# Cross-attention: the copy of the attended values out of PSUM moves from behind the fourth exponential of a step to behind the first exponential of the next

## The chip, the cores and the metric

The kernel runs on one core of one Trainium2 chip. The metric is the device time in microseconds (us); lower is better. The engines are called as in the profile: PE is TensorE, with PEld for its weight loads; ACT is ScalarE, DVE is VectorE, POOL is GpSimd, and SP is SyncE, which here only issues DMAs.

## The reference, cut to what matters

A decoder layer over 32 blocks of 128 positions and 512 features, in three parts: self-attention, cross-attention, feed-forward. The change touches the second alone:

```
qh = q.reshape(B, 8, 16, 512); kh = k.reshape(...); vh = v.reshape(...)
qk = einsum('bhdq,bhdl->bhql', qh, kh) * 0.25
ret = einsum('bhql,bhdl->bhdq', softmax(qk), vh)
x = layernorm(x + gamma * ret)
```

So each block has 8 heads of 512 queries, 512 keys and depth 16. The kernel never divides by the softmax's sum at this place. It computes exp(score - maximum), multiplies that by the values with a row of ones beside them, and the row of ones gives the sum.

## The kernel before

`self_attention`, `cross_attention` and `feed_forward` are three program blocks, one after the other: the second begins when all engines have left the first. In `cross_attention` every engine runs its own list of instructions, in order, and semaphores tie the lists together. [...]

A block of the batch is called t (0 to 31). It is worked off in 8 steps n = 0 to 7 (`STEPS`), four heads in steps 0 to 3 (group g = 0) and four in steps 4 to 7 (g = 1); within a group each step takes a quarter of the keys. `pairs` unrolls t = 0, 1 and t = 30, 31, and runs t = 2 to 29 in a hardware loop of 14 turns with two blocks in each, in which the values that waits compare with are computed from a register.

In step n the engines do this:

- PE (`step`, L1020 to L1036), in this order: a pair of score tiles k = 4n and 4n+1 into the PSUM buffers `e_ps` (two matmuls of L1017); the raw scores for the maximum of block t+1 (L981, two matmuls into `m_ps`); the third score tile; two more matmuls of L981; the fourth score tile; then `products(n - 1)` (L1002, eight records), which multiplies the exponentials of the step before by the values and adds into the one PSUM buffer `av_ps`. There are three buffers `e_ps` for four tiles a step (`bank_of`), so the pair of step n+1 waits until the third exponential of step n is done, and the fourth tile of step n waits until the first exponential of step n is done.
- ACT (`step`, L894 to L910): four exponentials of 128x512 (L901), from `e_ps` to `prob` in SBUF.
- DVE: two maxima (L926) over `m_ps`; at n = 5 also the reciprocals of the block before (L932, L936).

Steps 0 and 4 end with more. Behind `products`, PE transposes the maxima of one group into `m_ps` (L988); ACT copies them out (`evict_max`, L892); PE's next matmul of L981 waits for that copy, and so do POOL's splits (L852, L855) and the DMAs (L862) that bring the maxima to the stack `xs` for scores four steps later. ACT then copies the attended values of the group that has just been finished from `av_ps` to `heads` (`copy_heads`, L886). SP stores `heads` and later loads the sums for the reciprocals.

One wait counts above all:

```
if lc == 0 and not (first and g == 0):
    pe.wait_ge(heads_done, 2 * b + g)
```

`products` for the first quarter of a group overwrites `av_ps` and so waits for `copy_heads` of the group before. It stands at the end of PE's step 1 and of step 5. What `copy_heads` itself waits for is the `products` call at the end of PE's step 0 or 4, the last one of that group, and the store of the same `heads` buffer one block earlier.

Of the kernel before, what the change touches and what calls it, by code (L numbers as in the profile page):

```python
# [633 lines left out]
def cross_attention(nc, NB, t_in, scratch, ffn_stage, ffn_abs):  # L634
# [13 lines left out]
    def bank_of(k):  # L648
        return k % 3

    with ExitStack() as ctx:
# [62 lines left out]
        def pairs(eng, pair):  # L714

            pair(0, True, False)
            if NB > 4:
                with eng.Fori(1, NB // 2 - 1) as s:
                    pair(s, False, False)
            pair(NB // 2 - 1, False, True)  # L720
# [159 lines left out]
        @block.scalar  # L880
        def _(act):
            def copy_heads(b, g, first=False):
                act.wait_ge(av_done, STEPS * b + KC * (g + 1))
                if not first:
                    act.wait_ge(heads_st[g], 16 * b)
                act.activation(heads[g][:, :], av_ps[:, :], ACT.Copy).then_inc(heads_done, 1)  # L886

            def evict_max(b, g, first=False):
                act.wait_ge(mt_done, 2 * b + g + 1)
                if not first:  # L890
                    act.wait_ge(part_done, 4 * b + 2 * g - 2)
                act.activation(neg_max[g][:, :], m_ps[0][0:XG * KC, 0, 0:P], ACT.Copy).then_inc(neg_done, 1)  # L892

            def step(t, first, second=False, last=False):  # L894
                for n in range(STEPS):
                    for j in range(XG):
                        k = XG * n + j
                        act.wait_ge(score_done[k % 2], PAIRS * t + k // 2 + 1)
                        if j == 0 and not (first and n < 2):
                            act.wait_ge(av_done, STEPS * t + n - 1)  # L900
                        act.activation(prob[k % 8][:, :], e_ps[bank_of(k)][:, :], ACT.Exp, scale=0.25).then_inc(  # L901
                            exp_done, 1)
                    if n == 0:
                        evict_max(t, 1, first=first)
                    if n == 4 and not last:
                        evict_max(t + 1, 0)
                    if n == 0 and not first:
                        copy_heads(t - 1, 1, first=second)
                    if n == 4:
                        copy_heads(t, 0, first=first)  # L910

            def pair(s, first, last):
                step(2 * s, first)
                step(2 * s + 1, False, second=first, last=last)

            evict_max(0, 0, first=True)
            pairs(act, pair)
            copy_heads(NB - 1, 1)
# [948 lines left out]
```

## Time and profile before

| | us |
|---|---|
| median of 3 runs (1956.88 to 1959.33) | 1959.2 |
| the profiled execution | 1966.56 |
| its span, first to last instruction | 1964.7 |
| cross-attention in it, first to last exponential | 667.0 to 1393.1 |
| ACT busy, share of the span | 70% |
| PE busy, share of the span | 86% |

The profiled execution is 7.4 us above the median of the runs. A time difference that is read in the trace is taken off both alike.

### The profile page before, as it was taken

The page shows a single profiled execution, that of the slowest core. Times are in us where ns is not written, and L with a number is a line of the kernel's source. Part 1 is how long each engine was busy: PE and PEld are TensorE (multiplying, and loading weights), DVE is VectorE, ACT ScalarE, POOL GpSimd, SP SyncE. Part 2 cuts the span into 40 slices and gives each one's busy share as a digit, 9 for nine tenths or more (in the row PEclk, how much of TensorE's full clock was granted, in tenths as well). Part 3 has the DMA queues.
Part 4 walks back from the last instruction along what each step waited for, and adds up shares of the span by engine and source line. Part 5 has one row for each costly group of instructions (what it writes and reads, how often), then busy time and mean ns, then how long its engine had stood idle before and what let it go on. Part 6 is the DMA issues. An engine that isn't in the chain of part 4 may idle for free. (4 is left out here: it accounts for less than half of the span.)

```text
span 1964.7 us, 40878 instructions
## 1 busy us (share of the span) xinstructions
PE 1684.6 (86%) x11428; PEld 922.5 (47%) x11492; DVE 1421.5 (72%) x1915; ACT 1378.4 (70%) x2861; POOL 849.0 (43%) x1378
## 2 busy tenths in 40 slices
PE   5999999999994699999999999998336777777776
PEld 4877777777773233333333333333113333333332
DVE  3555555555553788888888888887448999999986
ACT  4555555555552378787777777786529999999996
POOL 3466566556553322323223232232364554545542
PEclk8999999999997699999999999998558888888887
DMA  3333433433433554444444443444233333333311
GB/s 113 102 102 112 127 105 113 124 109 110 123 116 104 119 167 117 107 108 106 105 115 110 107 107 105 114 111 147 80 88 94 109 99 97 109 99 112 96 65 43
DMA packets 118563, 210.97 MB, mean 107 GB/s; under 512 B 32097, under 2 KB 34689, under 8 KB 116737
## 3 DMA queue, kind: packets, MB, share of 16 engines
q1 hardware_dynamic: 110338, 209.51, 37.5%
q0 software_dynamic: 8192, 1.07, 0.3%
q8 instruction: 14, 0.23, 0.0%
q14 instruction: 19, 0.16, 0.0%
HBM read 133.41 MB, written 76.02 MB: 107 GB/s over the span
## 5 line engine op out<-in xcount | busy, mean ns | idle before, releaser
L926 DVE TENSOR_REDUCE b_smax<-b_m 128x2 f32<-128x1024 f32 x512 | 602.7, 1221 | 111.6 <-PE b_m L981 109.9
L901 ACT ACTIVATE b_prob<-b_e 128x512 f32<-128x512 f32 x1024 | 528.1, 603 | 138.5 <-PE b_e L1017 138.4
L1017 PE MATMUL b_e<-b_xs,b_cs 50*128 50x512 f32 x1024 | 358.8, 477 | 19.6 <-DMA b_xs<-b_max_part 5.6
L1017 PEld LDWEIGHTS b_e<-b_xs,b_cs 50*128 50x128 f32 x1024 | 143.9, 187 | 305.9 <-ACT b_prob L901 274.5
L1002 PE MATMUL b_av<-b_prob,b_vT 128*32 128x512 f32 x2048 | 278.5, 617 | 0.0
L1775 PE MATMUL c_y_ps<-c_w,c_hqT 128*128 128x512 bf16 x481 | 175.8, 532 | 112.3 <-issue 104.5
L981 PE MATMUL b_m<-b_cs,b_xs 48*128 48x512 f32 x1024 | 236.1, 434 | 37.1 <-DMA b_gamma<-in_gamma 30.9
L852 POOL TENSOR_SCALAR b_max_part<-b_neg_max 16x128 fp32r<-16x128 f32 x64 | 18.4, 288 | 464.6 <-ACT b_neg_max L892 464.6
L362 ACT ACTIVATE a_prob<-a_bank,a_neg_max 128x128 f32<-128x128 f32 x512 | 179.5, 386 | 54.7 <-DVE a_neg_max L442 54.7
L1775 PEld LDWEIGHTS c_y_ps<-c_w,c_hqT 128*128 128x128 bf16 x512 | 64.0, 129 | 214.0 <-issue 190.9
L862 POOL DMA_DIRECT2D b_xs<-b_max_part x256 | 136.0, 537 | 43.7 <-POOL b_max_part L855 36.9
L981 PEld LDWEIGHTS b_m<-b_cs,b_xs 48*128 48x128 f32 x1024 | 117.6, 190 | 74.3 <-POOL b_vT L830 31.3
L524 PE MATMUL a_bank<-a_w_hi,a_xT_hi 128*128 128x512 f32 x384 | 115.2, 422 | 14.1 <-POOL a_xT_lo L259 14.1
L1763 PE MATMUL c_h<-c_w,c_xqT 128*128 128x512 bf16 x510 | 121.1, 393 | 0.7 <-issue 0.7
L442 DVE TENSOR_REDUCE a_neg_max<-a_bank 128x4 f32<-128x512 f32 x128 | 82.2, 684 | 53.1 <-PE a_bank L566 53.1
L362 ACT ACTIVATION_READ_ACCUMULATOR a_prob<-a_bank,a_neg_max 128x1 f32 x512 | 115.8, 226 | 0.0
L271 POOL TENSOR_TENSOR a_q_sin<-a_q_raw,a_sin 128x256 f32<-128x256 f32 x64 | 55.2, 883 | 131.9 <-ACT a_q_raw L332 131.9
L456 DVE TENSOR_TENSOR a_x_sum<-a_bank,a_x 128x512 f32<-128x512 f32 x32 | 22.1, 692 | 124.2 <-DMA a_x<-in_x 119.2
L524 PE MATMUL a_bank<-a_w_lo,a_xT_hi 128*128 128x512 f32 x384 | 104.6, 394 | 0.0
L524 PE MATMUL a_bank<-a_w_hi,a_xT_lo 128*128 128x512 f32 x384 | 103.1, 390 | 0.0
L332 ACT ACTIVATE a_q_raw<-a_bank 128x512 f32<-128x512 f32 x32 | 19.1, 598 | 107.4 <-PE a_bank L524 107.4
L524 PEld LDWEIGHTS a_bank<-a_w_hi,a_xT_hi 128*128 128x128 f32 x384 | 65.7, 191 | 35.3 <-issue 11.9
(149 smaller groups left out, 3142.3 us busy)
## 6 DMA issues: line engine op xcount, KB each, us to landing
scratch_c_part<-a_c_part SPq DMA_DIRECT2D x64, 256.0 KB
scratch_x_part<-a_x_part SPq DMA_DIRECT2D x64, 256.0 KB
b_xs<-scratch_x_part SPq DMA_DIRECT2D x128, 128.0 KB, 3.0
b_cs<-scratch_c_part SPq DMA_DIRECT2D x128, 128.0 KB, 3.0
scratch_heads<-b_heads SPq DMA_DIRECT2D x64, 256.0 KB, 2.4
a_xT<-in_xT SPq DMA_DIRECT2D x32, 256.0 KB, 5.1
a_c_in<-in_ctx SPq DMA_DIRECT2D x32, 256.0 KB, 2.6
a_x<-in_x SPq DMA_DIRECT2D x32, 256.0 KB, 5.3
```

Source lines behind the costliest of these rows:

```text
L271: pool.tensor_tensor(s3[:, :, e:DH:2], q3[:, :, 1 - e:DH:2], sin[:, e:DH:2].unsqueeze(1).broadcast_to([P, NH, DH // 2]), ALU.mult).then_in ...
L362: last = act.activation(prob[:, j, c, :], s_ps[j][:, c * P:(c + 1) * P], ACT.Exp, bias=neg_max[:, j, c:c + 1], accum_out=den[:, j, c:c + 1])
L442: dve.tensor_reduce(neg_max[:, j, :], s_ps[j][:, :].rearrange("p (c n) -> p c n", c=KC), AX.X, ALU.max, negate=True).then_inc(max_done, 1)
L524: last = pe.matmul(out, a[:, c, :], b[:, c, :], start=(n == 0), stop=(n == 3 * KC - 1))
L862: pool.dma_start(xs[p][g][row:row + 1, :, :].rearrange("r h q -> r (h q)").bitcast(F32), max_part[g][2 * KC * e:2 * KC * (e + 1), j, :].bi ...
L901: act.activation(prob[k % 8][:, :], e_ps[bank_of(k)][:, :], ACT.Exp, scale=0.25).then_inc(exp_done, 1)
L926: dve.tensor_reduce(smax[g][:, :, j, qc], m_ps[u % 2][:, :, :], AX.X, ALU.max, negate=True).then_inc(max_done, 1)
L981: last = pe.matmul(m_ps[u % 2][:, e, :], xs[p][g][half(e, STACK), j, qc * P:(qc + 1) * P], cs[p][g][half(e, STACK), j, :], start=True, sto ...
L1002: last = pe.matmul(av_ps[2 * XD * h:2 * XD * (h + 1), :], vT[p][:, lc, XG * g + h, :], prob[(XG * n + 2 * j + e) % 8][:, :], start=(lc == ...
L1017: pe.matmul(e_ps[bank_of(2 * u + e)][:, :], cs[p][g][half(e), j, lc * P:(lc + 1) * P], xs[p][g][half(e), j, :], start=True, stop=True).the ...
L1763: last = pe.matmul(h_ps[:, n, :], xqT[:, c, :], w1[:, c, n * D:(n + 1) * D], start=False, stop=(c == KC - 1))
L1775: last = pe.matmul(y_ps[:, :], hqT[:, c, :], w2[:, c, :], start=(c == 0), stop=(c == FC - 1))
```

## The change

`copy_heads` is called at the same two places of a block as before, once for each group, but later in ACT's order. Before, it stood behind `evict_max` at the end of steps 0 and 4, ahead of all exponentials of the next step. Now it stands inside step 1 and step 5, behind the first of the four exponentials. The waits of `copy_heads`, its size and its number are the same. Nothing changes on the other engines' lists.

```
@@ -900,14 +900,14 @@
                             act.wait_ge(av_done, STEPS * t + n - 1)
                         act.activation(prob[k % 8][:, :], e_ps[bank_of(k)][:, :], ACT.Exp, scale=0.25).then_inc(
                             exp_done, 1)
+                        if j == 0 and n == 1 and not first:
+                            copy_heads(t - 1, 1, first=second)
+                        if j == 0 and n == 5:
+                            copy_heads(t, 0, first=first)
                     if n == 0:
                         evict_max(t, 1, first=first)
                     if n == 4 and not last:
                         evict_max(t + 1, 0)
-                    if n == 0 and not first:
-                        copy_heads(t - 1, 1, first=second)
-                    if n == 4:
-                        copy_heads(t, 0, first=first)
```

## Rows read from the trace of the kernel before

**Rows 1.** The page: busy time, share of the span and instructions of each engine.

```profile
PE 1684.6 (86%) x11428; PEld 922.5 (47%) x11492; DVE 1421.5 (72%) x1915; ACT 1378.4 (70%) x2861; POOL 849.0 (43%) x1378
```

**Rows 2.** One turn of the loop: length; busy PE, PEld, DVE, ACT, POOL; clock; DMA.

```profile
1027.70:1072.30 44.60, 43.89 (x262) 17.05 (x260) 38.50 (x36) 35.49 (x73) 12.69 (x26) 1.00 0.44 109
```

**Rows 3.** Groups of ACT instructions by line, 736 to 1341 us.

```profile
L901 ACT ACTIVATE b_prob<-b_e 128x512 f32<-128x512 f32 x865 | 446.0, 603 | 103.1 <-PE b_e L1017 103.1
L886 ACT ACTIVATE b_heads<-b_av 128x512 f32<-128x512 f32 x54 | 31.2, 578 | 0.0
```

**Rows 4.** Who waited for whom, 736 to 1341 us: total us, times, longest.

```profile
PEld b_e L1017 <- ACT b_prob L901: 237.4, 378, 0.9
ACT b_prob L901 <- PE b_e L1017: 103.1, 163, 0.7
...
PEld b_m L981 <- DVE b_smax L926: 6.6, 27, 0.3
```

**Rows 5.** Timeline of block 16, step 6, a plain step: start, duration.

```profile
1043.89 0.50 PE L1017 MATMUL b_e<-b_xs,b_cs 50*128 50x512 f32 x2
...
1044.23 0.40 PE L981 MATMUL b_m<-b_cs,b_xs 48*128 48x512 f32 x2
...
1044.51 2.06 ACT L901 ACTIVATE b_prob<-b_e 128x512 f32<-128x512 f32 x4 [0.62 <-PE b_e L1017]
...
1045.16 0.18 PEld L1017 LDWEIGHTS b_e<-b_xs,b_cs 50*128 50x128 f32 x1 [0.50 <-ACT b_prob L901]
...
1045.58 0.16 PEld L1002 LDWEIGHTS b_av<-b_prob,b_vT 128*32 128x32 f32 x8 [0.24 <-issue]
...
1046.58 0.50 PE L1017 MATMUL b_e<-b_xs,b_cs 50*128 50x512 f32 x2
```

**Rows 6.** Timeline of block 16, step 5, with the small copy before it.

```profile
1040.99 0.50 PE L1017 MATMUL b_e<-b_xs,b_cs 50*128 50x512 f32 x2
1041.19 0.27 ACT L892 ACTIVATE b_neg_max<-b_m 16x128 f32<-16x128 f32 x1 [0.41 <-PE b_m L988]
1041.36 0.57 ACT L886 ACTIVATE b_heads<-b_av 128x512 f32<-128x512 f32 x1
1041.51 0.19 PEld L981 LDWEIGHTS b_m<-b_cs,b_xs 48*128 48x128 f32 x2 [0.33 <-ACT b_neg_max L892]
...
1041.84 2.05 ACT L901 ACTIVATE b_prob<-b_e 128x512 f32<-128x512 f32 x4
...
1041.85 0.61 PE L981 MATMUL b_m<-b_cs,b_xs 48*128 48x512 f32 x2
...
1042.47 0.18 PEld L1017 LDWEIGHTS b_e<-b_xs,b_cs 50*128 50x128 f32 x1 [0.44 <-ACT b_prob L901]
...
1042.90 0.16 PEld L1002 LDWEIGHTS b_av<-b_prob,b_vT 128*32 128x32 f32 x8 [0.24 <-issue]
```

**Rows 7.** PE timeline: score pairs of steps 1 and 2, 17's 1 and 2, 5 and 6.

```profile
1029.79 0.50 PE L1017 MATMUL b_e<-b_xs,b_cs 50*128 50x512 f32 x2
...
1032.73 0.50 PE L1017 MATMUL b_e<-b_xs,b_cs 50*128 50x512 f32 x2
...
1052.27 0.50 PE L1017 MATMUL b_e<-b_xs,b_cs 50*128 50x512 f32 x2
...
1055.08 0.49 PE L1017 MATMUL b_e<-b_xs,b_cs 50*128 50x512 f32 x2
...
1063.33 0.50 PE L1017 MATMUL b_e<-b_xs,b_cs 50*128 50x512 f32 x2
...
1066.24 0.50 PE L1017 MATMUL b_e<-b_xs,b_cs 50*128 50x512 f32 x2
```

**Rows 8.** Timeline of PE: pairs that waited for a DMA, blocks 2 and 30.

```profile
724.49 0.50 PE L1017 MATMUL b_e<-b_xs,b_cs 50*128 50x512 f32 x2 [0.50 <-DMA b_xs<-b_max_part]
...
1355.41 0.80 PE L1017 MATMUL b_e<-b_xs,b_cs 50*128 50x512 f32 x2 [4.23 <-DMA b_xs<-b_max_part]
```

**Rows 9.** Timeline of ACT in block 30, outside the loop, a plain step.

```profile
1349.04 1.09 ACT L901 ACTIVATE b_prob<-b_e 128x512 f32<-128x512 f32 x2 [0.54 <-PE b_e L1017]
```

## The prediction

> **What bounds the kernel now.** I read the page's busy times first [rows 1]: PE is busy for 86% of the span, ACT for 70%, and no engine is at its end everywhere. The three parts of the layer have separate limits, so I went to cross-attention alone, by the busy time of one turn of its loop [rows 2]. PE is busy for 43.89 of 44.60 us at a granted clock of 1.00, its higher level (2.4 GHz); ACT for 35.49, DVE for 38.50. That looks like a PE bound, but a busy PE record overlaps with the next, so the waits decide. The chain of waits [rows 4] names two engines that wait for each other: PE for ACT's exponentials 378 times and ACT for PE's scores 163 times. The timeline of a plain step shows how the ring closes [rows 5]; times are given from the start of the step's score pair (1043.89):
>
> - the first exponential starts at +0.62 (1044.51);
> - the fourth score tile starts at +1.27 (1045.16), 0.65 later: one exponential takes 0.60 [rows 3], and 0.05 passes until PE goes on;
> - the products start at +1.69 (1045.58), 0.42 later;
> - the next pair starts at +2.69 (1046.58), 1.00 later.
>
> So a step takes 2.69 us, and of ACT's four exponentials only the first lies on the ring. Four take 2.06 us, one every (2.06 - 0.60) / 3 = 0.49, so ACT stands idle for 0.62 us in each step [rows 5], and these idle times are 103.1 us in all [rows 3].
>
> Step 5 (and step 1, built alike) is longer [rows 6]. From its pair (1040.99): the small copy of the maxima starts at +0.20, the large copy of the attended values at +0.37, and the first exponential only at +0.85 instead of +0.62. The 0.23 goes through the ring undiminished: fourth tile +1.48, products +1.91, next pair +2.90 (1043.89). The four such steps in a turn of the loop take 1032.73 - 1029.79 = 2.94, 2.90, 1055.08 - 1052.27 = 2.81 and 1066.24 - 1063.33 = 2.91 [rows 5, 6 and 7], 11.56 us together, 0.80 above four plain steps.
>
> **The change, part by part.**
>
> *The copy leaves the place ahead of the first exponential.* The small copy starts at +0.20, and another instruction followed it after 0.17 (1041.36 - 1041.19) [rows 6]. ACT is then free at +0.37 and waits for the scores, so the first exponential starts at +0.62 as in a plain step. The fourth tile can follow at +1.27 as far as ACT is concerned. PE's own queue allows it only a little later: its matmuls of L981 wait for the small copy, and the last record of them ends at +1.47 (1041.85 + 0.61 - 1040.99) [rows 6]. A matmul starts before the one ahead of it has ended: in the plain step the next one starts 0.34 after a pair that lasts 0.50, 0.16 early [rows 5]. So the fourth tile can start between +1.27 and +1.31, and the products, 0.42 later, between +1.69 and +1.73. If PE did have to reach +1.47, nothing would be won by this part; the overlap speaks against that.
>
> *The copy comes in behind the first exponential.* ACT's next instruction starts 0.49 after the first, so the copy starts at +1.11. It takes 0.57 in [rows 6] and 0.578 as a mean [rows 3]; the ends are 0.57 and the 0.60 of an exponential, and I take 0.58. It ends at +1.69, and with the same 0.05 until PE sees it, the products, which wait for the copy because it empties their buffer, can start at +1.74. By the fourth tile alone they would start at +1.69 to +1.73. So up to 0.05 us is given back: before, the copy was over at +0.94 and nobody waited for it.
>
> *The three other exponentials are later by the copy's place.* The copy was followed by an instruction after 0.48 [rows 6]. The third exponential then starts at +0.62 + 0.49 + 0.48 + 0.49 = +2.08, ends 0.60 to 0.62 later, and frees PE's next pair at +2.75 at the latest. The products that start at +1.74 let the pair go at +1.74 + 1.00 = +2.74. Both agree within 0.01. The fourth exponential starts at +2.57, and ACT is free at about +3.05, ahead of the next first exponential at +2.74 + 0.62 = +3.36. So ACT's idle time covers the whole copy. Without that cover the copy would cost its 0.49 in each of those steps.
>
> *Others who wait for the copy.* SP's store of `heads` moves by 0.5 us or so; behind it on SP's queue stand the loads of the sums and of the next stacks, which are used several us later. The reciprocals at n = 5 wait for the sums of a copy made four steps before, 11 us. The maxima are not moved. DVE has 44.6 - 38.5 = 6 us to spare in a turn [rows 2], and PE waited for it only 6.6 us in 27 turns [rows 4]. No transfer is added.
>
> *Sum.* Such a step becomes 2.74 us. In one turn of the loop that is 11.56 - 4 x 2.74 = 0.60 us. The loop has 14 turns. In the first, PE's pair of block 2, step 4, waited 0.50 us for a DMA of the maxima [rows 8], and that swallows what was won before it, 0.20 of this turn; the same holds for blocks 0 and 1, and for step 1 of block 30 with its wait of 4.23. Block 31's two copies are worth some tenths, which I leave out. That gives 14 x 0.60 - 0.20 = 8.2 us. Against the profiled execution: 1966.56 - 8.2 = 1958.4; against the median of the runs, which is 7.4 lower, 1959.2 - 8.2 = 1951.0 us.
>
> The Trainium skill prices the copy a little higher. "ScalarE: Activation LUTs", section "What ACT_TABLE_LOAD costs", gives an activation with immediate scale 186 ns + 0.833 ns an element, 613 ns here, and says that neighbours overlap by 93 ns, so one starts every 520. This trace shows 490 and 578 [rows 3, 5]. By the page the copy would be seen by PE 0.07 later and the win would be about 4.4 us instead of 8.2, an estimate from that page; the trace's durations decide.
>
> **The rivals.**
>
> *The products never wait for the copy.* If the copy is quicker behind an exponential than I think, or PE needs longer to reach the products, those steps shrink to the plain 2.69. For it: 0.05 us is all that separates the cases. Against: the third exponential is late by the same copy and holds the pair to about +2.75 anyway. It would give 11.56 - 4 x 2.69 = 0.80 a turn, 14 x 0.80 less 0.25 = 11 us: 1948.2.
>
> *ACT's waits are not hidden, in part.* Inside the loop each wait compares with a value computed from a register. For a price: the idle time before the first exponential is 0.62 in the loop [rows 5] and 0.54 outside it [rows 9], so one more such wait behind a blocked one seems to cost 0.08. The copy brings two. If both were added ahead of the copy, it would end 0.16 later, the products would start at +1.90, and the step would be 2.90: no change, 1958 to 1959. Against it: the copy stands 0.17 behind the small copy today with the same two waits ahead of it [rows 6]. That is far inside the 0.49 that the exponential gives them.
>
> A sentence of the Trainium skill bears on this, "Perfetto Trace Analysis", section "DVE / Act Engine Instruction": the sequencer hands an instruction to a wait queue and goes on to decode the next while the engine works. By it those waits cost nothing; the 0.17 agrees.
>
> *The copy slows the ring, and the kernel gets slower.* The same mechanism at full price: two waits ahead of the copy and one ahead of the exponential behind it, all unhidden, put the third exponential's end at 2.75 + 0.24 = +2.99, and the pair waits for it. The step is then 2.99 against a mean of 2.89 today: 0.10 x 54 = 5.4 us lost, 1964.6. It begins to lose from 0.15 us of unhidden work per copy on. The 0.17 just named speaks against it, and so does the 0.49 between exponentials, each of which has a wait ahead of it.
>
> **How the numbers follow.** The forecast has 0.70, the products that never wait 0.12, the waits hidden in part 0.12, the slower case 0.06. The predicted time is the forecast's, 1951.0. Its own range goes with the copy at 0.57 to 0.62 and a tenth of a turn's loss by PE or DVE on either side: wins of 6 to 9.5 us, 1949.7 to 1953.2. For 8 in 10 I take it down to the rival with 11 us and the runs' own scatter, 1947.2, and up to where only a quarter of the win is left, 1957.3. A difference of 0.2% (3.9 us) is about what a measurement of this kernel can tell from no change. Faster by more than that: the forecast and the first rival, 0.82, and a little of the second, so 0.83; within it 0.11; slower 0.06.
>
> **What the profile of the changed kernel would show.** In steps 1 and 5 the first exponential starts 0.62 after the pair; the idle time before it appears again, while the copy's row stands between one exponential and three. ACT's idle time in front of L901 rises by some 54 x 0.25 us minus what the shorter span takes. PEld of L1002 starts 0.05 us after the end of the copy, named as waiting for ACT `b_heads` L886, which it never was before. The four long steps of a turn measure 2.74 each, and a turn 44.1 instead of 44.7 us. PE's waits for the small copy and DVE's work stay the same. The prediction is wrong if the copy starts more than 0.6 us behind the exponential (waits not hidden), if the fourth score tile starts later than +1.31 (PE's own work was the next limit), or if the win is taken back by waits for DMAs as in block 30.

## The result and the profile after

| | before | changed |
|---|---|---|
| median, 20 runs of each | 1967.49 us (1956.88 to 1968.86) | 1955.84 us (1949.26 to 1959.44) |
| the profiled execution | 1966.56 | 1954.42 |
| its span | 1964.7 | 1952.6 |

The ratio of the changed kernel to the one before is 0.9951, with a 95% interval of 0.994 to 0.9962: faster by 0.49%. The forecast win was 8.2 of 1959.2 us, 0.42%, which lies inside that interval (wins of 0.38% to 0.60%), near its lower end. The forecast time of 1951.0 us was 4.8 below the changed kernel's median: 1955.84 lies above the 1949.7 to 1953.2 that the prediction gave for its forecast, though within the 1947.2 to 1957.3 that it gave for 8 in 10. The win and the time have to be explained apart, and the time is the more instructive.

The trace of the changed kernel, seen from the same places. First the groups of ACT instructions from 736 to 1341 us [rows 3]: operation, tiles, count, then busy us and mean ns, then idle time before them.

```profile
L901 ACT ACTIVATE b_prob<-b_e 128x512 f32<-128x512 f32 x877 | 459.4, 605 | 89.9 <-PE b_e L1017 87.8
L886 ACT ACTIVATE b_heads<-b_av 128x512 f32<-128x512 f32 x55 | 32.5, 592 | 0.0
```

ACT does more in the same 605 us (877 exponentials instead of 865), and its idle time ahead of them is 13 us smaller. The prediction had expected that idle time to rise. It forgot the step behind. In the timeline below the last exponential of the long step ends 0.41 us after the next pair's start (1043.01 against 1042.60); before, it ended with it (1043.89) [rows 6]. So the idle time ahead of the next step's exponentials is 0.19 us instead of 0.62 [rows 5], and that loss is more than the 0.14 that reappears ahead of the long step's first exponential. A copy lasts 592 ns here, 578 before; it now follows an exponential instead of the small copy, but no run tests whether that is the reason. The Trainium skill, "ScalarE: Activation LUTs", section "What ACT_TABLE_LOAD costs", has 613 ns for it by its formula; the trace's mean stays below that.

The chain of waits over the same stretch [rows 4]: who waited for whom, total us, times, longest.

```profile
PEld b_e L1017 <- ACT b_prob L901: 217.6, 388, 0.9
ACT b_prob L901 <- PE b_e L1017: 87.8, 199, 0.7
...
PEld b_av L1002 <- issue: 20.8, 72, 0.4
PEld b_m L981 <- ACT b_neg_max L892: 16.3, 54, 0.3
PEld b_m L981 <- DVE b_smax L926: 11.4, 29, 0.4
PEld b_av L1002 <- ACT b_heads L886: 8.2, 27, 0.3
```

The last row is new, and it was the one to look for: PE's products now wait for the copy. The profile names the copy 27 times only, for step 5; in step 1 it puts the same wait down to "issue", as the timeline of step 1 below shows. PE's wait for ACT's exponentials fell by 20 us.

The timeline of block 16, step 5, against [rows 6]: start, duration.

```profile
1039.86 0.51 PE L1017 MATMUL b_e<-b_xs,b_cs 50*128 50x512 f32 x2
1040.05 0.27 ACT L892 ACTIVATE b_neg_max<-b_m 16x128 f32<-16x128 f32 x1 [0.41 <-PE b_m L988]
...
1040.46 0.60 ACT L901 ACTIVATE b_prob<-b_e 128x512 f32<-128x512 f32 x1
...
1040.71 0.62 PE L981 MATMUL b_m<-b_cs,b_xs 48*128 48x512 f32 x2
...
1040.96 0.59 ACT L886 ACTIVATE b_heads<-b_av 128x512 f32<-128x512 f32 x1
...
1041.11 0.18 PEld L1017 LDWEIGHTS b_e<-b_xs,b_cs 50*128 50x128 f32 x1 [0.21 <-ACT b_prob L901]
...
1041.43 1.58 ACT L901 ACTIVATE b_prob<-b_e 128x512 f32<-128x512 f32 x3
1041.60 0.16 PEld L1002 LDWEIGHTS b_av<-b_prob,b_vT 128*32 128x32 f32 x8 [0.30 <-ACT b_heads L886]
...
1042.60 0.50 PE L1017 MATMUL b_e<-b_xs,b_cs 50*128 50x512 f32 x2
...
1043.20 2.07 ACT L901 ACTIVATE b_prob<-b_e 128x512 f32<-128x512 f32 x4 [0.19 <-PE b_e L1017]
```

From the pair (1039.86) the first exponential starts at +0.60 (forecast +0.62, before +0.85), the copy at +1.10 (+1.11), it ends at +1.69 (+1.69), the fourth score tile starts at +1.25 (+1.27 to +1.31), the products at +1.74 (+1.74), the next pair at +2.74 (+2.74, before +2.90). PE's own queue was no limit: the two records of L981 end at 1041.33, and the fourth tile starts at 1041.11, ahead of that end.

Step 1 of the same block is a little different:

```profile
1028.83 0.50 PE L1017 MATMUL b_e<-b_xs,b_cs 50*128 50x512 f32 x2
...
1029.36 0.60 ACT L901 ACTIVATE b_prob<-b_e 128x512 f32<-128x512 f32 x1
...
1029.86 0.59 ACT L886 ACTIVATE b_heads<-b_av 128x512 f32<-128x512 f32 x1
...
1030.56 0.19 PEld L1002 LDWEIGHTS b_av<-b_prob,b_vT 128*32 128x32 f32 x8 [0.37 <-issue]
...
1031.59 0.50 PE L1017 MATMUL b_e<-b_xs,b_cs 50*128 50x512 f32 x2
```

Its first exponential starts at +0.53 already, 0.09 sooner than forecast. The copy ends at 1030.45, but PE loads the weights of the products only 0.11 later and multiplies 0.14 later, not 0.05. The two differences nearly cancel, and the step takes 2.76 us.

### The profile page after: what moved, and what is told of

It reads as the page before. It is cut to its first block and busy times, and to the rows that moved or that the text cites. A ratio compares the mean times of both kernels' runs of the same rounds, so it can differ in the third digit from the quotient of the medians.

```text
span 1952.6 us, 40850 instructions
## 1 busy us (share of the span) xinstructions
PE 1668.4 (85%) x11428; PEld 922.1 (47%) x11492; DVE 1419.8 (73%) x1915; ACT 1386.0 (71%) x2861; POOL 851.2 (44%) x1378
## 5 line engine op out<-in xcount | busy, mean ns | idle before, releaser
L901 ACT ACTIVATE b_prob<-b_e 128x512 f32<-128x512 f32 x1024 | 536.5, 605 | 121.4 <-PE b_e L1017 119.2
L1002 PE MATMUL b_av<-b_prob,b_vT 128*32 128x512 f32 x2048 | 276.2, 611 | 2.9
L981 PE MATMUL b_m<-b_cs,b_xs 48*128 48x512 f32 x1024 | 238.5, 439 | 35.6 <-DMA b_gamma<-in_gamma 29.5
L1775 PE MATMUL c_y_ps<-c_w,c_hqT 128*128 128x512 bf16 x481 | 170.1, 518 | 113.4 <-issue 104.7
L981 PEld LDWEIGHTS b_m<-b_cs,b_xs 48*128 48x128 f32 x1024 | 117.0, 191 | 80.2 <-POOL b_vT L830 29.9
```

The source lines that it names most:

```text
L981: last = pe.matmul(m_ps[u % 2][:, e, :], xs[p][g][half(e, STACK), j, qc * P:(qc + 1) * P], cs[p][g][half(e, STACK), j, :], start=True, sto ...
L1002: last = pe.matmul(av_ps[2 * XD * h:2 * XD * (h + 1), :], vT[p][:, lc, XG * g + h, :], prob[(XG * n + 2 * j + e) % 8][:, :], start=(lc == ...
L1775: last = pe.matmul(y_ps[:, :], hqT[:, c, :], w2[:, c, :], start=(c == 0), stop=(c == FC - 1))
```

## The experiments

Each kernel was timed against the kernel before on the same chip, in runs mixed with it. The loop part is the time from the first exponential of block 2 to that of block 30, read in the profiled execution of each; steps are medians over blocks 4 to 28, from score pair to score pair, even and odd blocks.

| | ratio to before, 95% interval | loop part, us | step 1 | step 5 | step 7 |
|---|---|---|---|---|---|
| before, first profile | | 627.5 | 2.94, 2.81 | 2.90, 2.90 | 2.80, 2.73 |
| changed, first profile | 0.9951, 0.994 to 0.9962 | 618.5 | 2.76, 2.76 | 2.74, 2.75 | 2.73, 2.73 |
| e1 changed again | 0.9934, 0.9914 to 0.9955 | 618.7 | 2.76, 2.76 | 2.75, 2.74 | 2.73, 2.73 |
| e2 unchanged again | 0.9986, 0.9971 to 1.0 | 627.1 | 2.94, 2.80 | 2.90, 2.89 | 2.80, 2.73 |
| e3 only step 1 | 0.9974, 0.9959 to 0.9989 | 624.1 | 2.76, 2.76 | 2.91, 2.90 | 2.80, 2.73 |
| e4 only step 5 | 0.9967, 0.9951 to 0.9983 | 622.0 | 2.94, 2.81 | 2.75, 2.75 | 2.73, 2.73 |
| e5 behind the second | 1.0096, 1.0071 to 1.0121 | 645.8 | 3.25, 3.25 | 3.24, 3.24 | 2.73, 2.73 |
| e6 three more waits | 0.9953, 0.9935 to 0.9971 | 620.0 | 2.76, 2.76 | 2.75, 2.75 | 2.73, 2.73 |
| e7 copy on DVE | 0.9993, 0.9978 to 1.0007 | 612.9 | 2.61, 2.61 | 2.68, 2.69 | 2.73, 2.73 |
| e8 weight loads spread | 0.9945, 0.9924 to 0.9965 | 618.9 | 2.76, 2.76 | 2.75, 2.75 | 2.73, 2.73 |
| e9 copy on DVE, sums later | 0.9925, 0.9904 to 0.9946 | 613.3 | 2.61, 2.61 | 2.68, 2.68 | 2.73, 2.73 |
| e10 early wait for the values | 0.9954, 0.9939 to 0.9968 | 618.6 | 2.76, 2.76 | 2.74, 2.75 | 2.73, 2.73 |
| e11 unchanged, third profile | | 627.4 | 2.94, 2.81 | 2.91, 2.89 | 2.80, 2.73 |

**e1 and e2: both kernels again.** No edit. They tell what belongs to the change and what to an execution. In the expectations, "ring theory" is the prediction's account, in which a step is as long as the chain of waits between PE and ACT; "edge theory" says that what executions of one kernel differ by lies outside the loop.

> The changed kernel once more, as it is. Ring theory: the two long steps of each block take 2.74 to 2.76 us between score pairs as in the first profile, one turn of the loop 44.1 to 44.2 us, and the loop part gives 8 to 9 us whatever the execution. Edge theory: what the executions differ by lies outside the loop (blocks 0, 1, 30, 31 and the feed-forward), up to 5 us either way, from waits for DMAs and a lower granted clock behind them. Rival: the change itself makes the longer wait in block 1 (total 26.8 us for block 1 against 23.0 before); then it must be there again in this trace.

> The kernel before, once more. No difference from itself within 0.3%. Its loop steps repeat to 0.01 us (2.94, 2.90, 2.81, 2.91 and one plain step of 2.80 in step 7 of even blocks). If block 1 again takes 23.0 us and the changed kernel again 26.8, the change has a cost at that place; if either varies, it is the execution's.

The loop repeats to 0.4 us in either kernel. Block 1, which took 26.82 us in the first profile of the changed kernel and 22.79 in that of the kernel before, took 23.32 in the changed kernel this time and 26.87 in the unchanged one. So that block's 4 us belong to the execution and not to the change. The kernel before against itself came out at 0.9986; a difference of 0.15% is thus as good as none here.

**e3 and e4: one half of the change each.** In e3 `copy_heads` moves from step 0 to step 1 and stays in step 4; in e4 it moves from step 4 to step 5 and stays in step 0.

```
e3:                        if j == 0 and n == 1 and not first:
                               copy_heads(t - 1, 1, first=second)
     ...
                       if n == 4:
                           copy_heads(t, 0, first=first)
e4:                        if j == 0 and n == 5:
                               copy_heads(t, 0, first=first)
     ...
                       if n == 0 and not first:
                           copy_heads(t - 1, 1, first=second)
```

> Only the copy of the second group is moved (step 1), the other stands where it was. Ring theory: step 1 becomes 2.76 in both kinds of blocks, from 2.94 and 2.81, so 0.18 + 0.05 = 0.23 a turn, 14 x 0.23 = 3.2 us, ratio 0.9984; step 5 keeps 2.90. Rival (only the total of both counts, or the gain comes from the registers of the loop's queue): no such split. If the 0.07 that step 7 of even blocks lost by is tied to step 5, it stays 2.80 here.

> Only the copy of the first group is moved (step 5). Ring theory: step 5 becomes 2.74 to 2.75 from 2.90, 0.31 a turn, 4.4 us, and step 7 of even blocks loses its extra 0.07 (another 1 us) if that came from DVE's reciprocals running against the late ring; ratio 0.9972 to 0.9977. Step 1 keeps 2.94 and 2.81. Rival: step 7's extra 0.07 belongs to step 1's copy and stays here.

The loop part falls by 3.2 us in e3 and by 5.3 in e4 (from the mean of the three unchanged ones, 627.3), 8.5 in sum, and by 8.7 with both. The halves add up, as the theory of a ring says. The third column of steps shows a term that the prediction did not have: step 7 of even blocks loses 0.07 us in e4 and in the full change, and keeps it in e3. By e3 and e4 alone it would hang on step 5's copy; e6 shows the same 0.07 us in another step with that copy's place unchanged.

**e5: the copy behind the second exponential.** Only `j == 0` becomes `j == 1` in both conditions.

> The copy stands behind the second exponential of steps 1 and 5 instead of the first. Ring theory: the copy starts 0.48 later, at +1.51 to +1.59 from the score pair, PE sees it at +2.16 to +2.22, the products start then, and the next pair 1.00 later: 3.16 to 3.22 us for each of the four long steps of a turn, 12.8 against 11.01 in the changed kernel and 11.56 before. That is 17 us more than before over the loop, ratio to before about 1.009. Rival (ACT has 0.6 us of idle time a step, so the copy fits anywhere in it): no change against the changed kernel, ratio 0.995.

The rival, that ACT's idle time takes the copy wherever it stands, is out by 1.5% of the time. The timeline of block 16, step 5:

```profile
1049.94 0.50 PE L1017 MATMUL b_e<-b_xs,b_cs 50*128 50x512 f32 x2
...
1050.54 1.08 ACT L901 ACTIVATE b_prob<-b_e 128x512 f32<-128x512 f32 x2
...
1051.19 0.49 PE L1017 MATMUL b_e<-b_xs,b_cs 50*128 50x512 f32 x1
1051.52 0.60 ACT L886 ACTIVATE b_heads<-b_av 128x512 f32<-128x512 f32 x1
1051.99 1.11 ACT L901 ACTIVATE b_prob<-b_e 128x512 f32<-128x512 f32 x2
1052.17 0.16 PEld L1002 LDWEIGHTS b_av<-b_prob,b_vT 128*32 128x32 f32 x8 [0.79 <-ACT b_heads L886]
...
1053.17 0.50 PE L1017 MATMUL b_e<-b_xs,b_cs 50*128 50x512 f32 x2
```

The fourth score tile is as early as in the changed kernel (+1.25). The products wait for the copy, which ends at 1052.12, and start 0.05 later; then 1.00 to the next pair, as in every step shown. One place later costs 0.49 us, four times a turn. The steps took 3.24 to 3.25 us, a little over the 3.16 to 3.22 expected, and the loop part is 18.5 us longer than in the kernel before.

**e6: three more waits ahead of every copy.** Each is for something that was done long before.

```
+                for s, at in ((score_done[0], PAIRS * b + 8 * (g + 1)), (score_done[1], PAIRS * b + 8 * (g + 1)), (vT_done, b + 1)):
+                    act.wait_ge(s, at)
                 act.wait_ge(av_done, STEPS * b + KC * (g + 1))
```

> Three more waits, each for something long done, stand ahead of every copy of the changed kernel. If ACT's queue works such waits off while the exponential runs, the copy still starts 0.49 after it and nothing changes, ratio as the changed kernel (0.993 to 0.995). If each costs the 0.08 us of the prediction's second rival, the copy starts up to 0.24 later, the long steps become 2.98, and the kernel is 13 us slower than the changed one, ratio about 1.000 to 1.002.

The long steps are unchanged to 0.01 us, and the copy still starts 0.49 us behind the exponential (line numbers are two higher in this kernel):

```profile
1037.55 0.60 ACT L903 ACTIVATE b_prob<-b_e 128x512 f32<-128x512 f32 x1 [0.15 <-PE b_e L1019]
1038.04 0.59 ACT L888 ACTIVATE b_heads<-b_av 128x512 f32<-128x512 f32 x1
...
1039.68 0.50 PE L1019 MATMUL b_e<-b_xs,b_cs 50*128 50x512 f32 x2
...
1040.36 2.06 ACT L903 ACTIVATE b_prob<-b_e 128x512 f32<-128x512 f32 x4 [0.25 <-PE b_e L1019]
```

The prediction's second and third rival fall with this: five waits ahead of the copy delay it no more than two. The sentence of the Trainium skill that was weighed there ("Perfetto Trace Analysis", section "DVE / Act Engine Instruction"), that the sequencer goes on while the engine works, agrees with this. The 1.4 us by which the loop part is longer lie in step 6 of even blocks (2.75 instead of 2.68) and in block 2 (22.8 us, 22.3 and 22.5 in the two profiles of the changed kernel). In that step 6, the last two rows, the first exponential starts 0.68 us after the pair instead of 0.61. That is what step 7 of even blocks showed in the kernel before. So the extra 0.07 us comes and goes with what stands on ACT's list and is not tied to one place in the ring; its cause was not found.

**e7 and e9: the copy on DVE.** ACT's two calls go, and DVE makes the copy ahead of its maxima in steps 1 and 5. In e9 DVE also sums the first feed-forward weight one step later in block 31.

```
+                dve.tensor_scalar(heads[g][:, :], av_ps[:, :], 1.0, None, ALU.mult).then_inc(heads_done, 1)
...
                 for n in range(STEPS):
+                    if n == 1 and not first:
+                        copy_heads(t - 1, 1, first=second)
+                    if n == 5:
+                        copy_heads(t, 0, first=first)
...
e9 only:
-                    if last and n in (0, STEPS - 1):
-                        m = min(n, 1)
+                    if last and n in (1, STEPS - 1):
+                        m = n // (STEPS - 1)
```

> The copy goes to DVE, at the start of steps 1 and 5, ahead of the maxima, where DVE stands idle for 0.7 to 0.8 us because PE's raw scores wait for ACT's small copy. Ring theory: it starts about when the score pair does, ends by +0.7, nobody waits for it, ACT's first exponential is at +0.54 to +0.62 and the products at +1.69: all four long steps are 2.69, a turn is 0.25 us shorter than in the changed kernel, 3.5 us in all, ratio to before 0.991 to 0.993. Rival (DVE is then too full: reciprocals and maxima are late and PE waits for them): DVE's waits grow and steps 2, 3, 6 and 7 become longer than 2.69.

> The copy on DVE as in the run before last, but in block 31 DVE sums the first feed-forward weight behind the copy of step 1 instead of ahead of it, where the 8.85 us of sums held up the copy and PE with it. Ring theory: the loop part stays at 613 us (5.7 less than in the changed kernel, 14.4 less than before), block 31 goes from 34.5 back to 21 us, and the ratio to before becomes 0.991 to 0.993. Rival: the sums now stand ahead of the copy of step 5, hold that up, and block 31 keeps 5 us or more of the loss.

In e7 the loop won more than expected and the kernel was not faster. The loop part is 5.7 us shorter than in the changed kernel, where 3.5 was expected: step 1 went to 2.61 and not to 2.69, because its first exponential starts at +0.53 here too. What the loop won was lost in block 31, which took 34.5 us instead of 20.8 to 23.5:

```profile
1357.75 8.85 DVE L955 TENSOR_REDUCE w_abs<-stage 128x1 f32<-128x2048 f32 x4
...
1366.53 0.68 DVE L915 TENSOR_SCALAR b_heads<-b_av 128x512 f32<-128x512 f32 x1
...
1367.35 1.08 PE L1002 MATMUL b_av<-b_prob,b_vT 128*32 128x512 f32 x4 [5.44 <-DVE b_heads L915]
```

The sums stood ahead of the copy in DVE's queue, and PE waited behind it, so DVE keeps to the order of its list even when the copy could start. With the sums behind the copy (e9), block 31 takes 21.7 us, and the kernel has the lowest ratio of all, 0.9925 (median 1948.37 us), though its interval overlaps with the changed kernel's; the loop part, 5.3 us shorter, is the firmer evidence. Its step 5 of block 16:

```profile
1032.45 0.50 PE L1017 MATMUL b_e<-b_xs,b_cs 50*128 50x512 f32 x2
1032.62 0.68 DVE L915 TENSOR_SCALAR b_heads<-b_av 128x512 f32<-128x512 f32 x1
...
1033.06 2.06 ACT L895 ACTIVATE b_prob<-b_e 128x512 f32<-128x512 f32 x4 [0.16 <-PE b_e L1017]
...
1033.71 0.50 PE L1017 MATMUL b_e<-b_xs,b_cs 50*128 50x512 f32 x1
1034.14 0.16 PEld L1002 LDWEIGHTS b_av<-b_prob,b_vT 128*32 128x32 f32 x8 [0.25 <-issue]
...
1035.14 0.50 PE L1017 MATMUL b_e<-b_xs,b_cs 50*128 50x512 f32 x2
```

The copy is over at +0.85, nobody waits for it, the products start at +1.69 and the pair at +2.69. This is the prediction's first rival (products that never wait), reached by another engine. The chain of waits from 736 to 1325 us shows whose free time paid: DVE waited 77.7 us for PE's raw scores in the same stretch before (159 times), and waits 36.3 now.

```profile
DVE b_smax L921 <- PE b_m L981: 36.3, 121, 0.5
...
PEld b_m L981 <- DVE b_smax L921: 24.3, 81, 0.4
```

PE's waits for DVE rose from 6.4 (6.6 over the slightly longer stretch of [rows 4]) to 24.3 us without a step becoming longer. In the step above, the fourth tile (1033.71) still followed the first exponential's end by 0.05 us.

**e8: the loads of the second weight spread over blocks 30 and 31** (on the changed kernel).

```
-                    weights[0] = (((1, 0), (1, 1)), ((1, 2), (1, 3)))
+                    weights = [(((1, 0),), ((1, 1),)), (((1, 2),), ((1, 3),))]
```

> The changed kernel with the four 1 MB loads of the second feed-forward weight issued one at a time over blocks 30 and 31 instead of two at a time in block 30. Edge theory: the 4 us wait for the maxima's DMA in block 30 comes from those loads being ahead of it; it shrinks to under 1 us, the lower clock behind it goes too, and 4 to 6 us are won on the changed kernel, ratio to before 0.990 to 0.992. Rival: the wait only moves to block 31, or the last load ends too late for DVE's sums, and nothing is won.

PE's wait in block 30, then the busy times from 1375 to 1384 us, in block 31:

```profile
1344.71 0.65 PE L1017 MATMUL b_e<-b_xs,b_cs 50*128 50x512 f32 x2 [2.33 <-DMA b_xs<-b_max_part]
```

```profile
1375.00:1384.00 9.00, 8.48 (x32) 2.37 (x32) 5.27 (x3) 4.16 (x8) 0.00 (x0) 0.50 0.28 107
```

The wait in block 30 shrank to 2.33 us, from 4.04 in the changed kernel, but not to under 1. Nothing was won, as the rival said, but not in the way it said. Blocks 30 and 31 took 25.3 and 25.0 us instead of 27.4 and 20.8; the two together took 50.3 us, against 48.2 and 49.8 in the two profiles of the changed kernel. In block 31 no score pair waited for a DMA. There the granted clock fell to its lower level (0.50 in the second row: length, busy time of PE, PEld, DVE, ACT and POOL, clock, DMA), and the last steps took 4.07 us instead of 2.60 to 2.76. The ratio is the changed kernel's.

**e10: PE's wait for the values moved** (on the changed kernel), to test why PE goes on 0.14 us behind the copy in step 1.

```
-                if n == 0:
-                    pe.wait_ge(vT_done, b + 1)
...
                         products(*before(s, p), STEPS - 1)
+                    if n == 0:
+                        pe.wait_ge(vT_done, t + 1)
```

> The changed kernel, with PE's wait for the values moved from between the two other waits of the products of step 1 to the end of step 0, where it is long met. In the changed kernel PE went on 0.14 us after the copy's end in step 1 and 0.05 after it in step 5, and this wait is what step 1 has more. If it costs the 0.09, step 1 goes from 2.76 to 2.67, step 5 stays 2.74, and the loop is 2.5 us shorter. Rival (the 0.09 has another cause, the step's place in the loop): 2.76 stays.

Step 1 stays 2.76 and the loop 618.6. That wait is not the cause. The traces of the changed kernel narrow it down: in blocks 1, 30 and 31, outside the hardware loop, PE multiplies 0.14 us or more behind the copy in step 5 as well, and in steps 1, 2, 3 and 7 of block 30 the first exponential starts at +0.53. So step 1 inside the loop behaves as the steps outside it do, and step 5 inside it is the one that differs, in both respects. Why is open.

**e11: the kernel before, profiled a third time.**

> The kernel before, one more profiled execution, to see which parts its executions differ in. Edge theory: the loop part is 627.0 to 627.5 us again, and what differs from the other two executions lies in blocks 0, 1, 30 and 31 and in the feed-forward, where the granted clock falls behind a wait for a DMA.

Its time was 1960.44 us. Here are the parts of three executions of the same kernel, from the starts of first exponentials:

| part, us | first profile | e2 | e11 |
|---|---|---|---|
| the execution's time | 1966.56 | 1963.38 | 1960.44 |
| up to the first exponential | 667.0 | 665.5 | 666.6 |
| blocks 0 and 1 | 46.3 | 50.7 | 47.3 |
| blocks 2 to 29 (the loop) | 627.5 | 627.1 | 627.4 |
| blocks 30 and 31 | 52.3 | 49.8 | 48.2 |
| behind the last exponential | 571.6 | 568.5 | 569.1 |

The loop differs by 0.4 us, the rest by up to 4.4. The busy time from 1335 to 1395 us, blocks 30 and 31, in the first profile and in e11 (length; PE, PEld, DVE, ACT, POOL; granted clock; DMA):

```profile
1335.00:1395.00 60.00, 52.01 (x266) 17.77 (x265) 42.84 (x35) 39.61 (x79) 10.31 (x22) 0.82 0.33 112
```

```profile
1335.00:1395.00 60.00, 47.47 (x271) 16.47 (x267) 43.20 (x35) 40.34 (x81) 10.87 (x23) 0.94 0.35 117
```

A granted clock of 0.82 is a mean of the two levels over that stretch. In all three executions PE first stands idle for 4.0 to 4.2 us, waiting for the maxima's DMA, as here in e11:

```profile
1355.70 0.80 PE L1017 MATMUL b_e<-b_xs,b_cs 50*128 50x512 f32 x2 [4.02 <-DMA b_xs<-b_max_part]
```

In the first profile the clock was at its lower level once more in block 31, where PE has no maxima to compute, and that block took 23.5 us instead of 20.8. The same 5 us in the first profile and in e11:

```profile
1385.00:1390.00 5.00, 4.74 (x20) 0.98 (x12) 2.55 (x2) 2.27 (x5) 0.00 (x0) 0.50 0.00 0
```

```profile
1385.00:1390.00 5.00, 4.09 (x26) 1.13 (x29) 1.69 (x1) 3.98 (x8) 0.00 (x0) 1.00 0.00 0
```

## Why the prediction was right or wrong

**The mechanism was right, and in step 5 to 0.01 us at every instruction.** *The copy leaves the place ahead of the first exponential*: the exponential came back to +0.60, and the fourth tile followed. *The copy comes in behind the first exponential*: it started at +1.10, ended at +1.69, and the products waited for it until +1.74. In step 1 the same chain holds, but its total is right within 0.02 us partly by luck: the first exponential came at +0.53, 0.09 sooner than forecast, and PE multiplied 0.14 behind the copy's end, 0.09 later than forecast. e3 and e4 show that each half works alone, e5 that it is the copy's place in the ring, and not ACT's load, that counts.

**Two terms of the sum were mis-sized, in opposite directions.** The step length of 2.74 holds for step 5 (2.742 and 2.748), and step 1 measured 2.76 in both kinds of blocks. That is 0.02 x 28 = 0.6 us less win. And the prediction left out step 7 of even blocks, 2.80 before and 2.73 after: 0.07 x 14 = 1.0 us more. In the trace of before its first exponential started 0.68 instead of 0.62 us after the pair. It goes in e4 and stays in e3, but e6 puts the same 0.07 into step 6 by three waits on ACT's list alone, so no part of the forecast accounts for it and the cause was not found; that it fell to the win's side is luck. The loop part fell from 627.3 to 618.6, 8.7 us; the forecast was 8.2.

**The step that failed is the last one of the sum: "against the median of the runs ... 1959.2 - 8.2 = 1951.0".** It took the median of three runs for the level of the kernel. The 20 runs of before that stand beside the changed kernel's have a median of 1967.49 us. Nine of them lie between 1956.88 and 1962.31, eleven between 1967.43 and 1968.86, none between. The three runs at hand, which are among these 20, had all fallen into the lower group, and the profiled execution, at 1966.56, was close to the upper one. The prediction noted that gap of 7.4 us and used it as a constant offset, when it was the sign of a second level. With 1967.49 in the sum's place the forecast would have been 1959.3, and too high by 3.5: the base was 8.3 us too low and the win, by the difference of the medians (11.7 us), 3.5 too small. The two errors offset each other in part, so the miss of 4.8 is smaller than the failed step. How much of the 11.7 is the change's is less sure than the loop's 8.7: the interval of the ratio, taken of 1967.49, is 7.5 to 11.8 us.

The levels go with the mean granted clock. Of the 29 runs of before beside e1, the eight at a mean clock of 0.919 to 0.921 took 1959.2 to 1962.2 us, two at 0.917 and 0.918 took 1963.5 and 1963.8, and the 19 at 0.912 to 0.916 took 1966.2 to 1972.1. Beside e8 the line is less clean: three runs of before at 0.918 took 1960.8, 1965.5 and 1967.3. The changed kernel's 20 runs leave no gap between 1949.26 and 1959.44 us, but go the same way with the clock: ten at 0.918 to 0.921 with a median of 1951.7, ten at 0.914 to 0.917 with a median of 1957.0. Set beside the two groups of before (medians 1960.8 and 1967.9, grouped by their times), the change is worth about 9.1 us at the one level and 10.9 at the other. The forecast of 1951.0 holds for the first level alone, where it misses by 0.7. e11 and the first profile, one execution near each level, differ by 0.1 us in the loop, by 4.1 us in blocks 30 and 31 and by 2.5 behind them. That the clock goes with the level does not show that it is the cause, and why a run falls into one or the other was not settled.

**The rivals.** *The products never wait for the copy* needed another engine (e9); on ACT they did wait. *ACT's waits are not hidden* and *the copy slows the ring* fell in e6. The first of the two is refuted: three further waits cost nothing in the steps where they stand. The ring can be slowed by the copy, as the latter said, but it takes a place 0.48 us later (e5) and not a few waits.

**What was expected of the profile.** Right: the four long steps within 0.02 us, a turn of 44.2 us (618.5 / 14) where 44.1 was forecast, the small copy's unchanged 16.3 us. Half right: the wait of L1002 for `b_heads`, which is named in step 5 and not in step 1. Wrong: that ACT's idle time would rise; it fell. The prediction had ACT free at +3.05, which is 0.49 after the start of the fourth exponential; an exponential lasts 0.60, and the last one ended at +3.15.

## What to carry to other kernels

In a ring between two engines that work in order, an instruction costs what it delays on the ring, whatever its engine's idle time: here the same copy cost 0.05 to 0.18 us more ahead of the first exponential than behind it, and 0.49 more behind the second than behind the first. Walk the ring instruction by instruction, then ask which engine stands idle just when the operation becomes possible; DVE did here, and the loop won 14.0 us that way instead of 8.7. Before a win of half a per cent is put on top of a time, look at whether the runs have one level: a profiled execution that differs from the runs by more than they differ among themselves is a warning.

## What the hardware showed that was not expected

- The kernel before ran in two groups of times 7 us apart (medians 1960.8 and 1967.9), and lower times went with mean granted clocks about 0.920, higher ones with about 0.915.
- In step 1 of every block PE multiplies 0.14 us behind the end of the copy it waited for, in step 5 inside the loop only 0.05, and not because of the wait that step 1 has more (e10).
- Three more waits that were already met, ahead of the copy, did not delay it (0.49 us behind the exponential with two and with five); an extra 0.07 us turned up in step 6 of even blocks instead (e6).
- The copy of 128x512 from PSUM takes 0.68 us on DVE and 0.59 on ACT.
- DVE's later maxima made PE wait 24.3 us in all without costing anything.
